# A longer gather ring, smaller count low parts and a re-ordered start of three layers in a graph network kernel

## The chip, the cores and the metric

One Trainium2 chip, one core of it. The time is device time in microseconds (us) of one execution. The engines are TensorE (PE), VectorE (DVE), ScalarE (ACT), GpSimd (POOL) and SyncE (SP); they run their own instruction streams and wait for each other on semaphores.

## The reference

625 nodes with rows of 512, 10000 edges (src, dst) sorted by dst, with a type and a weight. Four blocks, each `x = layernorm(x + block(x))`:

```python
# L0: relational, 3 edge types, 3 node types
agg = segment_sum(einsum(x, W_rel)[etype, src] + b_rel[etype], dst); h = relu(x @ W_self[ntype] + b_self[ntype] + agg)
# L1: three SAGE layers
agg = segment_sum(x[src], dst) / max(cnt, 1)
h = relu(layernorm(agg @ W_l[i].T + x @ W_r[i].T + b[i]) * g[i] + b2[i]); x = h + x
# L2: four GINE layers
m = relu(x[src] + edge_attr @ We + be); h = ((1 + eps) * x + segment_sum(m, dst)) @ W1 + b1
x = relu(relu(batchnorm(h)) @ W2 + b2)
# L3: SAGE and a gate
h = (segment_sum(x[src], dst) / max(deg, 1)) @ W_l + b + x @ W_r;  h = h * sigmoid(h)
```

## The kernel before, in words

Nodes lie in NT = 5 row tiles of R = 125. Edges lie in TE = 83 tiles of up to 128, TF = 54 of one kind and TL = 29 of another, each of which scatters to one row tile. A float32 product is made of parts: a value is split into a high part (ScalarE casts it to fp32r) and a low part (VectorE subtracts the high part from the value), and PE multiplies the parts. Weights pass through the buffer `w_stage`: SP loads a 128x512 piece, ScalarE casts it (`w_high`, L1045), VectorE makes its low part (`w_low`, L1391), both into one of two weight buffers W[0] and W[1]. SP loads the next weight's piece after the low part of the last one (`w_split`).

The stages in order, with the times of the profile:

- Set-up and the rows of the relational product, 0 to about 101 us. They are stored to HBM as `rel_rows`.
- Counts, about 101 to 153 us. PE multiplies one-hot matrices into a count matrix in PSUM: NCF = 3 blocks and then NCL = 5 blocks of tiles, 8 in all, each of which raises `c_used`. The result, copied to TC, is the adjacency matrix with counts. Its high part is AT[HI] and its low part AT[LO]. Only two blocks of 125x125 of the low part are used, and `block_max`, `block_row` and `block_words` find which. `low_blocks` (L834) transposes these two blocks through PE, the copy `count_low_blocks` (CLO, L1266) takes them to SBUF, and `mean_low` (L913) multiplies by them.
- First block, about 153 to 276 us. POOL gathers a tile's rows of `rel_rows` with one indirect DMA each (L633), in the order ORDER. ScalarE casts the gathered tile (`m_high`, L1135), VectorE subtracts (`m_low`, L1623, raises `m_made`), PE multiplies with the tile's one-hot matrix (L862, raises `m_free`). The first GA = 4 gathers land in H; the others in a ring of GR = 24 slots. Gather i of the ring waits for `m_made` of i - GR + 1; the early ones wait for `c_used` of (i + 1) // 4, since the slots overlay buffers of the count stage. Between the steps, PE multiplies x by the self weights (L797), one `fill` at a time, in the order that FILL_AT writes out, and the weights W4 to W7 are split at steps W4_AT = 4, 26, 48, 70. The one-hot matrices are made in NG = 21 groups of four tiles; groups from KEPT = 12 on are stored by ScalarE's queue (`s_store`, L1119) to HBM in this stage, for the GINE layers, and groups 0 to 11 are made again, four in each SAGE layer (`onehots_again`, L1587).
- A layer norm and SAGE layer l = 0 (276 to 341 us), layer l = 1 (341 to about 410), layer l = 2 (to 448). Per row tile: root of the variance on ScalarE (`root`, L1053, function Sqrt), reciprocal on VectorE, normalisation, transposes on PE (L663), the two weight products (L671), the bias (`z_bias`, L903), `mean_low` and the product with AT (`mean_tile`, L919, raises `o_done`). Of l = 2 VectorE makes statistics, the affine part, the residual, statistics again; then the parts of x for the GINE layers: high on ScalarE (L1278), low on VectorE (`part_low`, L1831). `set_lhs` (L1738) makes the eight chunks of a matrix that the GINE gathers use, four of them within the row tiles of l = 2.
- Four GINE layers, 448 to 905 us. Their gathers are PE products (L973) or indirect DMAs into a queue (`queue_rows`).
- Last layer, 905 to 968 us: layer norm (ScalarE waits for `w2_done` of all five tiles before it), transposes, products, means, and per tile a sigmoid on ScalarE (L1344, function Sigmoid) with the next root behind it. ScalarE loads a table (ACT_TABLE_LOAD) when the function changes from Sqrt to Sigmoid or back.

The order within an engine is that of the program; nothing is reordered.

## Time and profile before

| | |
|---|---|
| Median of 3 runs | 971.86 us (967.61 to 972.33) |
| Profiled execution | 970.5 us, span 968.6 us |
| Granted clock, mean | 0.921 |
| PE busy | 841.4 us (87% of the span), 3561 matmuls |
| VectorE busy | 712.1 us (74%) |
| ScalarE busy | 516.6 us (53%) |
| POOL busy | 281.5 us (29%) |
| First block, 153 to 276 us | PE busy 103.34 of 123 us, clock 0.91, POOL 61.16 us |
| GINE layers, 448 to 905 us | PE busy 431.51 of 457 us, clock 0.98 |

The rows of the profile below give the start and the duration of a group of instructions on one engine in us from the span's start, the line of the kernel, the output and input tiles, and in brackets the idle time of the engine before it and what ended that. "issue" means that the profile shows nothing that the engine waited for; "remote" is a releaser that it can't name. The clock of 1.0 is 2.4 GHz, of 0.50 is 1.2 GHz.

### The profile page before, as it was taken

What the parts mean: (1) busy time and instruction counts of PE and PEld (TensorE: products, weight loads), DVE (VectorE), ACT (ScalarE), POOL (GpSimd) and SP (SyncE); (2) the same over time, 40 slices, a digit from 0 to 9 for tenths busy, and PEclk for the clock granted to TensorE, in tenths of its full rate; (3) what the DMA queues carried; (4) which work ended last, traced back from release to release, by engine and by line L of the source; (5) the groups of instructions that cost most, each with busy time, mean ns of one, the idle gap of its engine ahead of it and who ended that gap; (6) DMA issues with size and microseconds to landing.
All of it is one profiled execution on the core that took longest, in us unless ns stands there. A gap on an engine that the chain in (4) does not pass through costs nothing.

```text
span 968.6 us, 13328 instructions
## 1 busy us (share of the span) xinstructions
PE 841.4 (87%) x3561; PEld 603.7 (62%) x3561; DVE 712.1 (74%) x1275; ACT 516.6 (53%) x986; POOL 281.5 (29%) x245
## 2 busy tenths in 40 slices
PE   2989779887869789995999989999999999999796
PEld 2667345655647567773665865667656766658664
DVE  8997825765876677786888668976799758986535
ACT  2376103544646241514786567755677557764445
POOL 3000653865200000015352075502654045520000
PEclk9989657989969799997999999999999999999898
DMA  5412454676433312208676077841978138860101
GB/s 113 142 38 87 115 161 154 178 225 193 151 99 157 129 45 64 84 26 217 148 187 180 3 202 179 200 119 33 240 177 217 37 108 197 178 165 1 43 1 53
DMA packets 59286, 122.20 MB, mean 126 GB/s; under 512 B 9096, under 2 KB 22698, under 8 KB 59221
## 3 DMA queue, kind: packets, MB, share of 16 engines
q0 software_dynamic: 20048, 52.18, 22.6%
q1 hardware_dynamic: 36581, 64.56, 22.6%
q10 hardware_dynamic: 2592, 4.61, 1.3%
q8 instruction: 38, 0.62, 0.3%
q14 instruction: 27, 0.22, 0.1%
HBM read 105.60 MB, written 15.73 MB: 125 GB/s over the span
## 4 chain that ended last, share of the span: by engine, by line
PE 67%; DVE 17%; ACT 8%; issue 5%; another core or an unknown queue 2%; DMA 1%; SPq 0%; ACTq 0%; DVEq 0%
PE ps L996 15%; PE ps L973 10%; PE ps L671 9%; PE ps L1012 6%; PE ps L1028 6%; PE ps L797 4%; PE ps L862 3%; PE ps L919 3%; PE ps L776 2%; PE ps L663 2%; ACT slot_recs L1090 2%; PE ps L765 2%; DVE z_parts L1864 1%; DVE w L1391 1%
## 5 line engine op out<-in xcount | busy, mean ns | idle before, releaser
L996 PE MATMUL ps<-z_parts,onehot_dst 128*125 128x512 f32 x664 | 205.2, 414 | 5.6 <-DVE z_parts L1864 2.9
L1864 DVE SCALAR_TENSOR_TENSOR z_parts<-ps,z_parts 128x512 fp32r<-128x512 f32 x216 | 147.9, 688 | 43.4 <-ACT z_parts L1296 31.0
L671 PE MATMUL ps<-w,xT 128*125 128x512 f32 x660 | 174.7, 419 | 5.1 <-DVE w L1391 5.1
L1296 ACT ACTIVATE z_parts<-ps 128x512 fp32r<-128x512 f32 x216 | 128.7, 597 | 80.9 <-PE ps L973 66.9
L973 PE MATMUL ps<-x_parts,gather_lhs 128*128 x432 | 142.4, 415 | 22.5 <-DVE x_parts L1831 12.1
L996 PEld LDWEIGHTS ps<-z_parts,onehot_dst 128*125 128x125 f32 x664 | 110.0, 186 | 72.8 <-issue 55.0
L671 PEld LDWEIGHTS ps<-w,xT 128*125 128x125 f32 x660 | 129.8, 200 | 37.7 <-issue 6.8
L639 POOL DMA_INDIRECT queued<-node_rows,srci x60 | 96.0, 1600 | 93.7 <-ACT queued L1245 76.8
L653 POOL TENSOR_TENSOR work<-x_cur,be_rows 125x512 f32<-125x512 f32 x20 | 25.5, 1282 | 317.7 <-ACT x_cur L1059 188.9
L973 PEld LDWEIGHTS ps<-x_parts,gather_lhs 128*128 128x128 f32 x432 | 80.3, 193 | 56.5 <-issue 40.2
L633 POOL DMA_INDIRECT gathered<-rel_rows,rowi x79 | 85.7, 1084 | 51.4 <-DVE gathered_parts L1623 22.0
L1864 DVE SCALAR_TENSOR_TENSOR z_parts<-queued,z_parts 128x512 fp32r<-128x512 f32 x116 | 79.6, 686 | 5.5 <-ACT z_parts L1296 4.6
L1623 DVE TENSOR_TENSOR gathered_parts<-gathered,gathered_parts 128x512 fp32r<-128x512 f32 x79 | 53.1, 689 | 36.1 <-ACT gathered_parts L1135 26.2
L1135 ACT CAST gathered_parts<-gathered 128x512 fp32r<-128x512 f32 x79 | 47.5, 618 | 49.4 <-PE ps L862 34.6
L1296 ACT ACTIVATE z_parts<-queued 128x512 fp32r<-128x512 f32 x116 | 72.5, 625 | 0.4 <-issue 0.2
L862 PE MATMUL ps<-gathered_parts,onehot_dst 128*125 128x512 f32 x166 | 56.6, 440 | 16.5 <-DVE gathered_parts L1623 12.2
L644 POOL DMA_INDIRECT queued<-node_rows,srci x56 | 58.6, 1046 | 17.1 <-issue 12.2
L797 PE MATMUL ps<-w,xT 128*125 128x512 f32 x180 | 55.4, 422 | 3.2 <-DVE eps_deg L1600 1.8
L1012 PE MATMUL ps<-x_parts,w 128*128 128x312 f32 (+1 forms) x384 | 58.0, 313 | 0.1
L1391 DVE TENSOR_TENSOR w<-w_stage,w 128x512 fp32r<-128x512 f32 x88 | 57.0, 686 | 1.4 <-ACT w L1045 1.3
L1012 PEld LDWEIGHTS ps<-x_parts,w 128*128 128x128 f32 x384 | 57.1, 194 | 1.0 <-issue 1.0
L1028 PE MATMUL ps<-w,xT 128*125 128x512 f32 x240 | 57.0, 397 | 0.0
(275 smaller groups left out, 1154.7 us busy)
## 6 DMA issues: line engine op xcount, KB each, us to landing
w_stage<-in_weights SPq DMA_DIRECT2D x88, 256.0 KB
onehot_dst<-onehot_rows SPq DMA_DIRECT2D x80, 250.0 KB
onehot_rows<-onehot_dst ACTq DMA_DIRECT2D x18, 250.0 KB
gather_lhs<-edge_src_rows SPq DMA_DIRECT2D x8, 432.0 KB, 7.4
node_rows<-work SPq DMA_DIRECT2D x20, 160.0 KB, 2.0
queued<-node_rows,srci POOLq DMA_INDIRECT x116
node_rows<-work SPq DMA_DIRECT2D x20, 90.0 KB, 2.0
rel_rows<-rel_rows_out SPq DMA_DIRECT2D x10, 160.0 KB, 1.9
```

What stands on the lines that cost most here:

```text
L633: gp.indirect_dma_start(G[place(i)][:, :], None, xr_d, bass.IndirectOffsetOnAxis(ap=rowi[:, t:t + 1], axis=0)).then_inc(gath[place(i)], 16)
L639: gp.indirect_dma_start(Q[k % QR][:, :], None, xb_d, row, compute_op=ALU.add)\
L671: mm = pe.matmul(ps[0:R, bank, :], lt[:, a, k, n * R:(n + 1) * R], w[:, b, k, :], start=first and k == 0 and (a, b) == THREE[0], stop=last ...
L797: mm = pe.matmul(ps[0:R, FBANK[i % 3], :], XT[:, a, k, n * R:(n + 1) * R], W[(NREL + t) % 2][:, b, k, :], start=k == 0 and (a, b) == THREE ...
L862: mm = pe.matmul(ps[0:R, d, :], S[:, i // SK % SR, i % SK, :], M[:, i % MR, a, :], start=False, stop=False, skip_group_check=True)
L973: mm = pe.matmul(ps[:, 5 + t % 3, :], L[:, t, :], XS[:, a, bass.ds(s, 1), :], start=a == HI, stop=a == LO)
L996: mm = pe.matmul(ps[0:R, d, :], S[:, j // SK % SR, j % SK, :], Z[:, g % ZR, a, :], start=False, stop=False, skip_group_check=True)
L1012: mm = pe.matmul(ps[:, HBANKS[i], 0:HC[h]], W[0][:, a, k, o * P:(o + 1) * P], GT[:, b, k, HC[0] * h:HC[0] * h + HC[h]], start=k == 0 and ( ...
L1028: mm = pe.matmul(ps[0:R, n, :], XT[:, a, k, n * R:(n + 1) * R], W[1][:, b, k, :], start=False, stop=k == KT - 1 and (a, b) == THREE[-1])
L1296: nc.scalar.activation(Z[:, g % ZR, HI, :], of, ACT.Relu).then_inc(z_hi, 1)
L1391: v.tensor_tensor(W[j % 2][:, LO, k, :], WS[:, k, :], W[j % 2][:, HI, k, :].bitcast(F32), ALU.subtract).then_inc(w_split, 1)
L1864: v.scalar_tensor_tensor(out=Z[:, g % ZR, LO, :], in0=of, scalar=0.0, in1=Z[:, g % ZR, HI, :].bitcast(F32), op0=ALU.max, op1=ALU.subtract) ...
```

## The change

- The first GA = 12 gathers get places of their own, four in H and eight in the weight buffer W[0] (of GR = 30 ring slots, six more lie in the region of AT). The first twelve share a semaphore in pairs. Gathers whose slot is free before the counts end wait for `c_used` of i // 5; the six in AT's region wait for all 8 count blocks; the first that waits for `m_made` is the one at i = 42.
- W4's split begins at step 14 of the first block (W4_AT), with a wait of ScalarE for twelve gathers subtracted.
- KEPT = 9: nine one-hot groups are made again, three in each SAGE layer, and three more are stored during the first block.
- The whole low part of AT is no longer made. `low_blocks` transposes two blocks of the counts themselves (TC, bank 6) and two of the high part (bank 7), four matmuls, and VectorE makes CLO from them by a copy and a subtraction, right after `w_lows(8)`. `low_blocks` comes before `z_bias`.
- `set_lhs` of chunks 4 to 7 moves from the row tiles of l = 2 to the end of l = 1, between the calls y(2, 2), y(2, 3) and y(2, 4).
- At the end of l = 2 ScalarE casts tiles 0 to 3 before the last tile's second root, and VectorE makes the low part of tile 0 before the last tile's scale.
- A spare Sqrt on one column stands ahead of the first layer norm, a spare Sigmoid behind each root of the last tiles.
- ScalarE's wait for `w2_done` ahead of the last layer norm is gone.
- The queue's landings in the GINE layers use the gathers' semaphores.

```diff
...
 NCL = -(-TL // CL)
-GA = 4
-GR = 24
+GA = 12
+GR = 30
+GX = 3
 MR = 4
...
 AHEAD = 2
-KEPT = 12
+KEPT = 9
 MADE = [KEPT * i // NL1 for i in range(NL1 + 1)]
 DEG_AT = 4
-W4_AT, W5_AT, W6_AT, W7_AT = 4, 26, 48, 70
+W4_AT, W5_AT, W6_AT, W7_AT = 14, 26, 48, 70
 FILL_AT = [0] + [6 + j * 62 // 14 for j in range(1, NREL * NT)]
...
         G += [at(g_at, 2048 * (i if i < 7 else 9), f"gathered{13 + i}", [P, D]) for i in range(8)]
-        G += [at(x_at, 2048 * i, f"gathered{21 + i}", [P, D]) for i in range(GR - 21)]
-        G = [at(h_at, 2048 * (i + 1), f"first_gathered{i}", [P, D]) for i in range(GA)] + G
+        G += [at(x_at, 2048 * i, f"gathered{21 + i}", [P, D]) for i in range(GX)]
+        G += [at(a_at, 2048 * i, f"gathered{21 + GX + i}", [P, D]) for i in range(GR - 21 - GX)]
+        G = [W[0][:, i // KT, i % KT, :].bitcast(F32) for i in range(2 * KT)] + G
+        G = [at(h_at, 2048 * (i + 1), f"first_gathered{i}", [P, D]) for i in range(NT - 1)] + G
+        assert len(G) == GA + GR and 2048 * (GR - 21 - GX) <= APAD * 4
         assert AHEAD * 4096 <= 4 * CG * P and MR * 4096 <= g_off and g_off + 2048 * 13 <= 52224 and TF * P * 4 + 2048 * (QR + 2) <= 52224
...
         xr_last = sem("last_rel_rows_stored")
-        gath = [sem(f"gathered{i}_in") for i in range(GA + GR)]
+        gath = [sem(f"gathered{i}_in") for i in range(GA // 2 + GR)]
         m_hi = sem("m_hi")
...
         TCK = TC[:, :, :].rearrange("p s (d n) -> p (s d) n", n=R)
-        ATL = AT[:, LO, :, :].rearrange("p s n -> p (s n)").bitcast(F32)
+        ATH = AT[:, HI, :, :].rearrange("p s n -> p (s n)").bitcast(F32)
+        TCF = TC[:, :, :].rearrange("p s n -> p (s n)")
         TCB = TC[:, :, :].rearrange("p s (d n) -> p (s d) n", n=R)
...
 
+        def arrival(i):
+            return i // 2 if i < GA else GA // 2 + (i - GA) % GR
+
+        def queue_landed(l, k):
+            before = (TE - GA - 1 - k % QR) // GR + 1
+            return 16 * (before + l * ((TL - 1 - k % QR) // QR + 1) + k // QR + 1)
+
         def landed(i):
-            return 16 if i < GA else 16 * ((i - GA) // GR + 1)
+            return 32 if i < GA else 16 * ((i - GA) // GR + 1)
 
...
                     gp.wait_ge(m_made, i - GR + 1)
-                elif i >= 3:
-                    gp.wait_ge(c_used, min((i + 1) // 4, NCF + NCL - 1))
+                elif i >= GA + 21 + GX:
+                    gp.wait_ge(c_used, NCF + NCL)
+                elif i >= 4:
+                    gp.wait_ge(c_used, min(i // 5, NCF + NCL - 1))
                 gp.indirect_dma_start(G[place(i)][:, :], None, xr_d,
-                                      bass.IndirectOffsetOnAxis(ap=rowi[:, t:t + 1], axis=0)).then_inc(gath[place(i)], 16)
+                                      bass.IndirectOffsetOnAxis(ap=rowi[:, t:t + 1], axis=0)).then_inc(gath[arrival(i)], 16)
             def queue_rows(l, k):
...
                 pe.wait_ge(low_made, 3)
-                pe.wait_ge(at_made, NT)
+                pe.wait_ge(at_hi, NT)
                 for j in range(2):
                     b = field(low_word(j), 6, 31, NB - 1)
-                    mm = pe.matmul(ps[0:R, 6, P * (j + 2):P * (j + 2) + R], ident[0:R, 0:R],
-                                   ATL[0:R, bass.ds(b * R, R)], start=True, stop=True)
+                    for bank, rows in ((6, TCF), (7, ATH)):
+                        mm = pe.matmul(ps[0:R, bank, P * (j + 2):P * (j + 2) + R], ident[0:R, 0:R],
+                                       rows[0:R, bass.ds(b * R, R)], start=True, stop=True)
                 mm.then_inc(low_done, 1)
...
                             block_row()
+                    low_blocks()
                     z_bias(l, False)
-                    low_blocks()
                     mean_low(l)
-                    pe.wait_ge(at_hi, NT)
                     for n in range(NT):
...
             def m_high(t):
-                act.wait_ge(gath[place(t)], landed(t))
+                act.wait_ge(gath[arrival(t)], landed(t))
                 if t >= MR:
...
                     nc.scalar.copy(DGR[:, :], DG[:, :]).then_inc(dgr_made, 1)
+                if t == W4_AT:
+                    act.wait_ge(m_made, GA)
                 if t in range(W4_AT, W4_AT + 8, 2):
...
                     w_high(7, (t - W7_AT) // 2)
+            nc.scalar.activation(spare[:, :], epst[:, :], ACT.Sqrt)
             act.wait_ge(deg_made, 1)
...
                 if l == 0:
-                    act.wait_ge(low_done, 3)
-                    nc.scalar.copy(CLO[0:R, :, :], ps[0:R, 6, 2 * P:4 * P].rearrange("p (j n) -> p j n", n=P)[:, :, 0:R])\
-                        .then_inc(clo_made, 1)
                     act.wait_ge(z_done, 1)
...
             top = NT * NL1
+            def part_high(n):
+                nc.scalar.copy(XS[0:R, HI, n, :], X[0:R, n, :]).then_inc(xs_hi, 1)
+
             for n in range(NT):
                 root(n, top + FIRST[n], epsd)
+                if n == NT - 1:
+                    act.wait_ge(o_done, NT * NL1)
+                    act.wait_ge(x_made, NT * NL1 + NT - 1)
+                    for m in range(NT - 1):
+                        part_high(m)
                 root(NT + n, top + SECOND[n])
                 normal(X[0:R, n, :], H[0:R, n, :], NT + n, NT + n + 1, x_made)
-            act.wait_ge(o_done, NT * NL1)
-            for n in range(NT):
-                act.wait_ge(x_made, NT * NL1 + n + 1)
-                nc.scalar.copy(XS[0:R, HI, n, :], X[0:R, n, :]).then_inc(xs_hi, 1)
+            act.wait_ge(x_made, NT * NL1 + NT)
+            part_high(NT - 1)
 
...
                     else:
-                        c = l * ((TL - 1 - (t - TF) % QR) // QR + 1) + (t - TF) // QR + 1
                         if (t - TF) % 2 == 0:
-                            act.wait_ge(q_in[(t - TF) % QR], 16 * c)
+                            act.wait_ge(q_in[(t - TF) % QR], queue_landed(l, t - TF))
                         else:
...
                             nc.scalar.activation(X[0:R, n - 1, :], ps[0:R, n - 1, :], ACT.Relu).then_inc(x_kept, 1)
-            act.wait_ge(w2_done, NT * NL2)
             normed_rows(NL1, NT * (NL1 + 2), 2 * NT, XM_L3)
...
                 root(n, NT * (NL1 + 3) + n + 1)
+                nc.scalar.activation(spare[:, :], epst[:, :], ACT.Sigmoid)
 
...
 
+            def low_rows(bank):
+                return ps[0:R, bank, 2 * P:4 * P].rearrange("p (j n) -> p j n", n=P)[:, :, 0:R]
+
             def onehots_again(g):
...
             v.sem_inc(low_made, 1)
-            for s in range(NT):
-                v.wait_ge(at_hi, s + 1)
-                v.tensor_tensor(AT[:, LO, s, :], TC[:, s, :], AT[:, HI, s, :].bitcast(F32),
-                                ALU.subtract).then_inc(at_made, 1)
-                if s == 1:
-                    v.wait_ge(low_done, 1)
-                    v.tensor_reduce(bmx[:, :], ps[0:NB, 6, 0:R], AX_X, ALU.max).then_inc(low_made, 1)
+            v.wait_ge(low_done, 1)
+            v.tensor_reduce(bmx[:, :], ps[0:NB, 6, 0:R], AX_X, ALU.max).then_inc(low_made, 1)
             block_words()
             w_lows(8)
+            v.wait_ge(low_done, 3)
+            link(v.tensor_copy(CLO[0:R, :, :], low_rows(7)))
+            v.tensor_tensor(CLO[0:R, :, :], low_rows(6), CLO[0:R, :, :].bitcast(F32), ALU.subtract).then_inc(clo_made, 1)
             for g in range(MADE[0], MADE[1]):
...
             w_lows(11)
-            for n in range(2, NT):
-                y(2, n)
+            y(2, 2)
+            set_lhs(4)
+            set_lhs(5)
+            y(2, 3)
+            set_lhs(6)
+            set_lhs(7)
+            y(2, 4)
 
...
                 stats(H[0:R, n, :], NT + n)
-                if n < NT - 1:
-                    set_lhs(LCH // 2 + n)
+                if n == NT - 1:
+                    part_low(0)
                 scale(NT + n, NT * NL1 + SECOND[n])
-            for n in range(NT):
+            for n in range(1, NT):
                 part_low(n)
...
                     v.wait_ge(web_in, 16 * (l + 1))
-                v.wait_ge(q_in[k % QR], 16 * (l * ((TL - 1 - k % QR) // QR + 1) + k // QR + 1))
+                v.wait_ge(q_in[k % QR], queue_landed(l, k))
                 v.scalar_tensor_tensor(out=Q[k % QR][:, :], in0=WEB[:, :], scalar=wt[:, TF + k:TF + k + 1],
```

## Rows read from the trace of the kernel before

**Rows 1.** Page, part 4: the chain that ended last, share of span.
```profile
PE 67%; DVE 17%; ACT 8%; issue 5%; another core or an unknown queue 2%; DMA 1%; SPq 0%; ACTq 0%; DVEq 0%
```

**Rows 2.** Timeline of PE in the first block, its three long waits.
```profile
199.18 1.21 PE L862 MATMUL ps<-gathered_parts,onehot_dst 128*125 128x512 f32 x2 [4.07 <-issue]
...
225.72 1.21 PE L862 MATMUL ps<-gathered_parts,onehot_dst 128*125 128x512 f32 x2 [4.37 <-DVE gathered_parts L1623]
...
242.47 1.21 PE L862 MATMUL ps<-gathered_parts,onehot_dst 128*125 128x512 f32 x2 [3.12 <-DVE gathered_parts L1623]
```

**Rows 3.** Timeline of PE at the low blocks of layer l=0.
```profile
317.76 1.42 PE L903 MATMUL ps<-bias_parts,deg_rows 34*125 34x512 f32 x5
319.11 0.70 PE L834 MATMUL ps<-adjT,ident 125*125 x4
325.24 1.68 PE L913 MATMUL ps<-x_parts,count_low_blocks 125*125 x2 [5.43 <-issue]
```

**Rows 4.** Timeline of PE at the first GINE gather.
```profile
448.28 1.65 PE L973 MATMUL ps<-x_parts,gather_lhs 128*128 x3 [12.05 <-DVE x_parts L1831]
```

**Rows 5.** Timeline of PE in the last layer.
```profile
907.26 0.65 PE L663 MATMUL ps<-ident,work 125*128 125x125 f32 x4 [2.45 <-ACT work L1069]
...
957.35 2.49 PE L919 MATMUL ps<-x_parts,adjT 125*125 125x512 f32 x10
```

**Rows 6.** Timeline of POOL, count stage: start, us, [idle before, releaser].
```profile
126.75 0.95 POOL L633 DMA_INDIRECT gathered<-rel_rows,rowi  x1 [0.30 <-issue]
...
150.40 0.94 POOL L633 DMA_INDIRECT gathered<-rel_rows,rowi  x1 [1.34 <-remote]
```

**Rows 7.** Page, part 5: busy, mean ns, idle before and its releaser.
```profile
L1135 ACT CAST gathered_parts<-gathered 128x512 fp32r<-128x512 f32 x79 | 47.5, 618 | 49.4 <-PE ps L862 34.6
```

**Rows 8.** Windows: us, busy us (x instructions) per engine, PEclk, DMA, GB/s.
```profile
123.00:132.00 9.00, 5.09 (x30) 3.12 (x30) 0.16 (x1) 0.95 (x2) 3.78 (x4) 0.50 0.54 157
132.00:138.00 6.00, 5.25 (x34) 3.53 (x34) 2.72 (x8) 0.00 (x0) 3.80 (x4) 0.50 0.52 145
223.00:232.00 9.00, 6.28 (x22) 4.98 (x23) 5.67 (x10) 4.63 (x9) 4.92 (x5) 0.81 0.39 117
325.30:331.00 5.70, 5.59 (x13) 4.00 (x14) 1.73 (x3) 0.76 (x2) 0.00 (x0) 0.50 0.57 184
408.00:415.00 7.00, 6.61 (x22) 5.00 (x22) 3.54 (x6) 3.05 (x5) 0.00 (x0) 0.76 0.41 150
908.00:915.00 7.00, 4.97 (x15) 4.08 (x16) 4.75 (x12) 4.95 (x9) 0.00 (x0) 0.53 0.00 0
```

**Rows 9.** Timeline of ScalarE at the first layer norm.
```profile
278.06 1.28 ACT L1053 ACT_TABLE_LOAD   x1 [5.80 <-DVE mv L1668]
```

**Rows 10.** Timeline of VectorE at the end of layer l=2.
```profile
436.11 0.70 DVE L1738 TENSOR_SCALAR gather_lhs<-gather_lhs,pidx,pone 128x864 fp32r<-128x864 f32 x1
...
441.84 0.16 DVE L1683 RECIPROCAL rstd<-sd 125x1 f32<-125x1 f32 x1 [0.36 <-ACT sd L1053]
...
443.59 3.76 DVE L1831 TENSOR_TENSOR x_parts<-x_cur,x_parts 125x512 fp32r<-125x512 f32 x5 [1.39 <-ACT x_parts L1278]
```

**Rows 11.** Timeline of ScalarE at the last sigmoid.
```profile
958.73 1.28 ACT L1344 ACT_TABLE_LOAD   x1
960.02 0.69 ACT L1344 ACTIVATE x_cur<-ps,rdeg 125x512 f32<-125x512 f32 x1
```
**Rows 12.** Timeline of ScalarE at the low blocks.
```profile
323.62 0.37 ACT L1266 CAST count_low_blocks<-ps 125x250 fp32r<-125x250 f32 x1 [11.70 <-DVE onehot_dst L1587]
```

**Rows 13.** Timeline of VectorE at y(2,3).
```profile
403.17 0.75 DVE L1677 SCALAR_TENSOR_TENSOR x_parts<-ps,rdeg,x_parts 125x512 fp32r<-125x512 f32 x1 [1.59 <-ACT x_parts L1064]
```

**Rows 14.** Timeline of ScalarE at the end of layer l=2.
```profile
442.96 2.68 ACT L1278 CAST x_parts<-x_cur 125x512 fp32r<-125x512 f32 x5
```

**Rows 15.** Timeline of VectorE ahead of the last layer.
```profile
900.73 0.18 DVE L1668 BATCH_NORM_AGGREGATE mv<-st 125x2 f32<-125x6 f32 x1
```

**Rows 16.** Timeline of ScalarE at the start of the last layer.
```profile
904.85 0.29 ACT L1053 ACTIVATE sd<-mv,epst 125x1 f32<-125x1 f32 x1 [8.47 <-PE ps L1028]
```

More of the change, by code:

```diff
@@ L275, in build @@
         zero = sb("zero", [P, P], BF16)
+        spare = sb("spare", [P, 1])
         one2 = sb("one2", [2, ND], F32R)
@@ L389, in build @@
         q_set = sem("queue_rows_set")
-        q_in = [sem(f"queue{i}_in") for i in range(QR)]
+        q_in = gath[GA // 2:GA // 2 + QR]
         x_kept = sem("x_kept")
```

3 lines of the change are left out of this document (1 added, 2 removed).

## The prediction

> **What bounds the kernel now.** I read the chain that ended last first. [rows 1] gives 67% of it to TensorE (PE) and only 17% and 8% to VectorE (DVE) and ScalarE (ACT). So a saving counts only where PE stands idle. The four GINE layers, nearly half of the span, are left as they are by the diff, and nothing is to be had there. Next I read PE's own rows for those whose bracket shows an idle time: three of 3 to 4.4 us in the first block [rows 2], 5.43 us ahead of the low blocks' product [rows 3], 12.05 us ahead of the first GINE gather [rows 4], 2.45 us at the start of the last layer [rows 5]. The diff has an edit near each. Last came the rows of the engine that each bracket names. The profiled execution took 970.5 us (span 968.6 and 1.9 around it), 1.4 under the median of 971.86. All terms are against 970.5, and 1.4 is added back at the end.
>
> **Gathers and the ring (A, 0).** Twelve gathers instead of four get landing places of their own, and the ring has 30 slots instead of 24, so 42 gathers instead of 28 can go out before the first one that waits for `m_made`. A gather costs POOL 0.95 us with 0.30 of issue, 1.25 [rows 6], so 14 are 17.5 us of POOL's time. They are worth something only where a gather is late. In the first block ScalarE's casts of gathered rows idle 49.4 us, 34.6 of it for PE [rows 7], and PE's matmuls on them name VectorE's subtraction [rows 2]; nothing names a landing. The extra lead hides what is hidden. W4 moves from step 4 to step 14, since gathers lie in W[0] until then: four casts, four subtractions and SP's four loads, with W5's loads behind them on SP's queue. The step length is 122/83, 1.5 us; W4's last part is then subtracted at step 24 and W4 is first used at step 25 or 26, so only a step or two lie between; PE takes each step after VectorE's part of it, and that order hides it. W5 is cast from step 26 as now. ScalarE's new wait at step 14 (for `m_made`) has its next casts queued behind it, and PE waits for those, but 12 subtractions are done by step 14 anyway. The three one-hot stores more are issues on ScalarE's queue in the same idle time. All this is costed at nothing; if the cover were gone, a late gather would cost up to its 1.25 us, a late weight part about one step, 1.5.
>
> What may not be free is the form of the stream. Now 15 gathers go out in a row, until 127.7 us, and after that POOL rests 1.34 us after each few [rows 6]. In the 9 us around the end of that run PE did 30 matmuls; in the next 6 us it did 34, in 5.25 us of busy time [rows 8]. At the latter's pace 30 take 5.3 us, so 3.7 us went, with the clock at 0.50 in both. The new pacing (one count block per five gathers) makes the run nearly unbroken. I take zero, as the row that names the waiter in the first block never names a gather; the bounds are 11.6 less (the first block's three waits of 4.07, 4.37 and 3.12 vanish [rows 2]) and 18 more. Both are rivals below.
>
> **Square-root table (D, -1.1).** The ACT_TABLE_LOAD at 278.06 lasts 1.28 us and stands between VectorE's first variance and the root, after 5.80 idle us [rows 9]. A spare root ahead of that wait moves the load into the idle time: 1.28 + 0.3 are hidden by 5.80, and would cost the same 1.6 if ScalarE came late. The gain is 1.28 at most, 0.6 if the root then meets VectorE inside an operation of 0.7 [rows 10]; I take 1.1. The Trainium skill, "ScalarE: Activation LUTs", section "What ACT_TABLE_LOAD costs", adds a drain of 1.38 us to each switch, 2.66 in all; by that page the gain would be about 2.5 and the sum 1.4 lower. The trace disagrees: behind the load at 958.73 the sigmoid starts at 960.02, 0.01 us after the load's end [rows 11].
>
> **Low blocks (B, -5.3).** Now: z's bias 317.76 to 319.18, `low_blocks` from 319.11, 0.70, then PE idles 5.43 until 325.24 [rows 3]. What is late is the copy of CLO, ScalarE's 0.37 us at 323.62. Its data is there at 319.81, but it stands behind the `s_store` of the fourth remade one-hot, which its bracket names [rows 12]. After: VectorE makes CLO itself, right behind w_lows(8), and three one-hots per layer instead of four come behind CLO. AT's low part on VectorE, five subtractions, is gone. `low_blocks` is four matmuls, 2 x 0.70 = 1.4, and stands ahead of z's bias. Step by step: z ends 317.8; low blocks until 319.2; copy and subtraction, 0.4 each by ScalarE's 0.37 on the same shape, until 320.0, hidden by z's bias (1.42, until 320.6). From CLO's end, 323.99, to the product PE took 1.25, so it starts at 321.2, 4.0 earlier. Bounds: 3.4, if the two operations take 0.7 each as those of 512 do, and 4.6, if PE's own 1.25 overlaps the bias. The idle time has a second price: PE's clock is 0.50 from 325.3 to 331.0, 5.7 x 0.50 = 2.85 us of work lost; after the shorter gap ahead of the same product in layer l=2 it is 0.76 over 7 us, 1.7 lost [rows 8]. So 1.2 to 1.3 more, from 0 to 2.4. Sum 5.3, from 3.4 to 7. VectorE's chain of the layer starts at the end of each tile's means, which move whole.
>
> **Layer l=2 per tile (C, -2.5).** This stretch runs at VectorE's pace. `set_lhs`, 0.70, stands in four tiles ahead of the reciprocal, but the last tile, which has none, still waits 0.36 for ScalarE's root there [rows 10]: removing it saves about 0.17 per tile, 0.7 in all. It moves to between y(2,2), y(2,3) and y(2,4), in pairs of 1.4 us, where VectorE idles 1.59 [rows 13] and then about as long again: free, but with 0.2 us to spare; uncovered, up to 1.4 per pair. At the end of the layer ScalarE now casts five tiles, 442.96 to 445.64 [rows 14], VectorE subtracts five, 443.59 to 447.35, 0.75 each [rows 10], and PE starts at 448.28 [rows 4]. After, four casts come ahead of the last tile's root and part_low(0) ahead of its scale: 0.75 in a wait of 0.36, so 0.39 late. Scaled: 442.2 + 0.39 - 0.7 = 441.9; four subtractions, 3.0, until 444.9. The fifth cast starts at 442.96 - 0.3 and ends 443.2, in time. 447.35 - 444.9 = 2.45. What could be late is the root itself, behind four casts of 0.54 on ScalarE, 2.1 us; they fit if the tile before is normalised early enough, and cost up to 2.1 if not. Bounds 0.4 and 3.2 (the subtractions follow the casts at once).
>
> **The last layer's wait (F, -3.0).** VectorE has the first tile's variance at 900.91 [rows 15], but ScalarE's root starts at 904.85, held by `w2_done` of all tiles, PE's L1028 [rows 16]. Without the wait the root runs near 901, and normalising and scaling go beside PE's product, so PE's idle 2.45 ahead of 907.26 [rows 5] goes whole. The clock from 908 to 915 is 0.53, 3.3 us lost [rows 8]; a shorter gap gives part of that back, but VectorE still makes tiles at its own pace. I take 2.45 + 0.55; bounds 1.5 (VectorE's statistics are next) and 4.
>
> **Spare sigmoid (E, +0.8).** In the final tiles ScalarE alternates between two tables. From the second tile on the load stands right behind the root and ends as the sigmoid begins: 958.73, 1.28, then 960.02. PE has finished the last mean tile at 959.84 [rows 5], 0.2 before, so ScalarE sets the pace. A spare activation is one more on it, 0.29 as the small root of [rows 16], some 0.2 with overlap, four times. Nothing hides it if ScalarE is the pace. Bounds 0 (the wait for VectorE's variance hides it) and 1.2.
>
> **Sum.** 970.5 - 1.1 - 5.3 - 2.5 - 3.0 + 0.8 = 959.4; + 1.4 = 960.8. With all terms at one bound: 971.9 - 4.7 = 967.2 (0.6 + 3.4 + 0.4 + 1.5 - 1.2) and 971.9 - 15.5 = 956.4 (1.3 + 7 + 3.2 + 4).
>
> **Rivals.** (1) The forecast, 956.4 to 966. Chance 0.55.
> (2) The longer run of gathers slows PE in the count stage as the first one did. 15 cost 3.7; 27 more at that rate cost 6.7: 967.5, no change. For: 30 against 34 matmuls [rows 8]. Against: PE may have waited for a row there and not for the memory. Chance 0.10. The Trainium skill, "DMA: Bandwidth & Descriptors", section "SWDGE vs HWDGE vs iDMA", says that GpSimd writes its descriptors to rings in SBUF that VectorE can lock it out of, which would hurt POOL, not PE; the rows show only that the two coincide.
> (3) The other side. Every nine gathers or so without a rest bring one stall of the kind that the first block shows, and the 27 more put three into it: 4.37 of wait and (1 - 0.81) x 9 = 1.7 of clock [rows 2, 8], 18.2 in all: 979.0, slower. It decides from 15.9 us, 5.3 each. Against: POOL runs ahead and rests there. Chance 0.05.
> (4) With the lead, POOL is never in a hurry in the first block, and the three waits vanish: 960.8 - 11.6 = 949.2. For: one of them is "issue", none a landing [rows 2], so what holds them is not in the data flow. Against: then nothing shows that it is POOL. Chance 0.15.
> (5) The gaps of PE close but open again on VectorE and ScalarE, so half of B, C and F comes: 960.8 + 5.4 = 966.2. For: C's and F's stretches are at VectorE's pace. Against: at B what follows is released by PE. Chance 0.15.
>
> **Range and chances.** The likeliest time is 960.8. The range goes from 949.0 (rival 4) to 967.5 (rivals 2 and 5); beyond it lie rival 3 and the outer parts of 2 and 4. A change of 0.5%, 4.9 us, is about what can be told from none: faster is below 967.0, slower above 976.7. Faster: 0.55 + 0.15 + 0.12 of rival 5 + 0.03 of rival 2 = 0.85; same 0.10; slower 0.05.
>
> **What would show it.** In the profile after: no table load between the first variance and its root; the low blocks' product with an idle of about 1 us and a clock above 0.6 behind it; the first GINE gather with an idle near 9.5; the last layer's first transpose with no idle; the final tiles 0.2 us longer each. The prediction is wrong if the count stage or the first block moves by more than 3 us: a slower PE from 120 to 150 (2, 3), or the three waits gone (4).

## The result and the profile after

The changed kernel takes 958.57 us (median of 4 runs, 953.77 to 961.46); the kernel before took 972.10 us beside it. The ratio is 0.988, with a 95% interval of 0.984 to 0.992, so 8 to 16 us came off. The profile below is of an execution of 953.77 us (span 951.9), the fastest of the four. It is 16.7 us shorter than the profiled one of before, more than the medians differ by, so a second trace of the same kernel (span 957.4 us) stands beside it from here on.

First the chain that ended last, share of the span, of the changed kernel:

```profile
PE 70%; DVE 16%; ACT 7%; issue 6%; DMA 0%; ACTq 0%; SPq 0%; DVEq 0%
```

PE's share rose from 67% [rows 1] to 70%; the gaps went and the work stayed. This table gives the stages between marks of PE's timeline in the traces, in us:

| Stretch, from PE's marks | before | after | after, 2nd trace |
|---|---|---|---|
| second part of the counts: its first matmul to the first scatter | 35.64 | 41.66 | 43.92 |
| first block: first to last scatter | 116.07 | 106.30 | 114.75 |
| last scatter to the low blocks' product | 50.39 | 43.56 | 43.82 |
| low blocks' product to the last mean of l=0 | 15.60 | 13.44 | 13.41 |
| layers l=1 and l=2 to their last mean | 95.39 | 94.84 | 95.20 |
| last mean of l=2 to the first GINE gather | 12.05 | 9.87 | 9.91 |
| GINE layers, to the end of the last weight product | 456.53 | 458.13 | 452.64 |
| from there to the first mean of the last layer | 32.13 | 27.88 | 27.41 |
| means of the last layer | 22.90 | 22.90 | 22.90 |
| last mean to the end | 8.76 | 9.13 | 9.14 |

Every stretch with an edit moved, and so did two that the forecast had at zero: the counts got 6 to 8 us longer and the first block 1 to 10 us shorter. The GINE layers, where nothing was changed, differ by 5.5 us between two traces of the same program; all fourteen traces lie between 452.5 and 458.1. That much is chance there, and the rest of the table is to be read with it in mind.

The low blocks on PE, in the changed kernel:

```profile
312.89 0.38 PE L849 MATMUL ps<-counts,ident 125*125 x2
...
313.85 1.43 PE L918 MATMUL ps<-bias_parts,deg_rows 34*125 34x512 f32 x5
315.76 0.49 PE L928 MATMUL ps<-x_parts,count_low_blocks 125*125 x1 [0.48 <-issue]
```

And on VectorE, whose two operations follow at once:

```profile
313.96 0.42 DVE L1795 CAST count_low_blocks<-ps 125x250 fp32r<-125x250 f32 x1 [1.65 <-PE ps L849]
314.41 0.42 DVE L1796 TENSOR_TENSOR count_low_blocks<-ps,count_low_blocks 125x250 fp32r<-125x250 f32 x1
```

The idle time of 5.43 [rows 3] is 0.48. Four windows of the changed kernel, beside [rows 8]:

```profile
123.00:132.00 9.00, 4.84 (x26) 2.60 (x26) 0.00 (x0) 1.14 (x2) 6.87 (x8) 0.50 0.72 212
132.00:138.00 6.00, 1.49 (x7) 0.73 (x7) 0.25 (x1) 0.00 (x0) 2.27 (x4) 0.50 0.60 173
...
315.80:321.50 5.70, 5.27 (x22) 4.02 (x23) 4.52 (x9) 2.48 (x5) 0.00 (x0) 1.00 0.68 235
...
892.00:899.00 7.00, 4.87 (x20) 3.82 (x19) 4.75 (x12) 5.01 (x9) 0.00 (x0) 0.76 0.00 0
```

Behind the low blocks the granted clock is 1.00 where it was 0.50, in the last layer 0.76 where it was 0.53. In the count stage PE did 26 matmuls in 9 us and then 7 in 6 us, where it had done 30 and 34. POOL meanwhile, in the changed kernel:

```profile
133.92 0.95 POOL L647 DMA_INDIRECT gathered<-rel_rows,rowi  x1 [0.30 <-issue]
137.99 0.97 POOL L647 DMA_INDIRECT gathered<-rel_rows,rowi  x1 [3.12 <-PE ps L790]
```

The one at 133.92 is the twentieth in a row since 104.20. POOL rests as PE's count comes late, and PE is at full pace again when POOL has rested. All this while PE's waits are "issue", so no row names what holds it.

The first block's long waits in this trace are 1.58 and 2.75 us, in place of 4.07, 4.37 and 3.12 [rows 2]:

```profile
211.13 0.72 PE L877 MATMUL ps<-gathered_parts,onehot_dst 128*125 128x512 f32 x2 [1.58 <-DVE gathered_parts L1645]
214.60 1.21 PE L877 MATMUL ps<-gathered_parts,onehot_dst 128*125 128x512 f32 x2 [2.75 <-DVE gathered_parts L1645]
```

The second trace of the same kernel has them at their old size:

```profile
208.90 1.21 PE L877 MATMUL ps<-gathered_parts,onehot_dst 128*125 128x512 f32 x2 [4.33 <-DVE gathered_parts L1645]
...
248.51 1.21 PE L877 MATMUL ps<-gathered_parts,onehot_dst 128*125 128x512 f32 x2 [3.81 <-DVE gathered_parts L1645]
```

So of the 9.8 us by which the first block is shorter in the first trace the second one keeps 1.3; what part is chance takes more traces ("The old gathers"). The first layer norm, the end of l=2 and the start of the last layer on PE, in the changed kernel:

```profile
277.94 1.09 PE L677 MATMUL ps<-ident,work 125*128 125x125 f32 x4 [2.54 <-ACT work L1083]
...
281.92 4.04 PE L685 MATMUL ps<-w,xT 128*125 128x512 f32 x12
...
433.91 2.49 PE L987 MATMUL ps<-x_parts,gather_lhs 128*128 x5 [9.87 <-DVE x_parts L1856]
...
891.88 0.59 PE L677 MATMUL ps<-ident,work 125*128 125x125 f32 x4
894.60 0.76 PE L677 MATMUL ps<-ident,work 125*128 125x125 f32 x4 [2.13 <-ACT work L1083]
```

The last layer's first transpose has no idle time (2.45 before [rows 5]); the second has 2.13, as before.

### The profile page after: what moved, and what is told of

The parts are those of the page before. It is cut to its first block, busy times and chain, and to the rows that moved or that the text cites. A ratio compares the mean times of both kernels' runs of the same rounds, so it can differ in the third digit from the quotient of the medians.

```text
span 951.9 us, 13338 instructions
## 1 busy us (share of the span) xinstructions
PE 835.9 (88%) x3565; PEld 600.8 (63%) x3565; DVE 707.6 (74%) x1269; ACT 519.1 (55%) x992; POOL 278.0 (29%) x245
## 4 chain that ended last, share of the span: by engine, by line
PE 70%; DVE 16%; ACT 7%; issue 6%; DMA 0%; ACTq 0%; SPq 0%; DVEq 0%
PE ps L1010 15%; PE ps L685 10%; PE ps L987 10%; PE ps L1026 6%; PE ps L1042 6%; PE ps L811 4%; PE ps L877 4%; PE ps L934 3%; PE ps L790 3%; PE ps L677 2%; DVE z_parts L1889 2%; PE ps L779 2%; DVE w L1410 1%; ACT z_parts L1315 1%; ACT slot_recs L1104 1%
## 5 line engine op out<-in xcount | busy, mean ns | idle before, releaser
L685 PE MATMUL ps<-w,xT 128*125 128x512 f32 x660 | 171.2, 412 | 4.9 <-DVE w L1410 4.9
L685 PEld LDWEIGHTS ps<-w,xT 128*125 128x125 f32 x660 | 126.9, 196 | 36.6 <-issue 6.6
L647 POOL DMA_INDIRECT gathered<-rel_rows,rowi x71 | 72.8, 1026 | 43.9 <-DVE gathered_parts L1645 19.5
L877 PE MATMUL ps<-gathered_parts,onehot_dst 128*125 128x512 f32 x166 | 54.5, 424 | 10.4 <-DVE gathered_parts L1645 9.6
L1645 DVE TENSOR_TENSOR gathered_parts<-gathered,gathered_parts 128x512 fp32r<-128x512 f32 x71 | 47.7, 690 | 19.2 <-ACT gathered_parts L1149 16.2
L1149 ACT CAST gathered_parts<-gathered 128x512 fp32r<-128x512 f32 x71 | 42.7, 618 | 33.9 <-PE ps L877 26.4
L1026 PE MATMUL ps<-x_parts,w 128*128 128x312 f32 (+1 forms) x384 | 60.4, 321 | 0.1
L1026 PEld LDWEIGHTS ps<-x_parts,w 128*128 128x128 f32 x384 | 59.5, 202 | 0.5 <-issue 0.5
L1059 ACT CAST w<-w_stage 128x512 fp32r<-128x512 f32 x88 | 50.5, 616 | 14.6 <-DVE onehot_dst L1606 9.9
L811 PE MATMUL ps<-w,xT 128*125 128x512 f32 x180 | 54.8, 418 | 3.2 <-DVE eps_deg L1622 1.8
```

Of the source, the lines that this page charges most:

```text
L647: gp.indirect_dma_start(G[place(i)][:, :], None, xr_d, bass.IndirectOffsetOnAxis(ap=rowi[:, t:t + 1], axis=0)).then_inc(gath[arrival(i)], 16)
L685: mm = pe.matmul(ps[0:R, bank, :], lt[:, a, k, n * R:(n + 1) * R], w[:, b, k, :], start=first and k == 0 and (a, b) == THREE[0], stop=last ...
L811: mm = pe.matmul(ps[0:R, FBANK[i % 3], :], XT[:, a, k, n * R:(n + 1) * R], W[(NREL + t) % 2][:, b, k, :], start=k == 0 and (a, b) == THREE ...
L877: mm = pe.matmul(ps[0:R, d, :], S[:, i // SK % SR, i % SK, :], M[:, i % MR, a, :], start=False, stop=False, skip_group_check=True)
L1026: mm = pe.matmul(ps[:, HBANKS[i], 0:HC[h]], W[0][:, a, k, o * P:(o + 1) * P], GT[:, b, k, HC[0] * h:HC[0] * h + HC[h]], start=k == 0 and ( ...
```

## The experiments

Four sets ran on different chips: the first four kernels on one where the kernel before took 975.0 us, the next four on one with 974.5, the three after that on one with 947.8, and the last on one with 950.7. Comparisons between kernels are made within a set, and between sets only where said.

### The changed kernel again

Edit: none.

> The changed kernel once more, for a second trace of it. Theory A (each saving lies in a stall that the edit removes): the product of the low blocks stands near 316, the first GINE gather near 434, the last transpose near 892, each within 3 us. Rival N (a part of the 16.6 us by which the two traces differ is chance of one execution): the count stage, the first block or the GINE layers differ between the two traces of the same program by 3 us or more.

Measured: 958.8 us (958.39 to 961.58), ratio to before 0.987 (0.980 to 0.995); its stages are the table's last column. The marks that the theory named lie 11, 11 and 6 us late. The 11 come from the counts and the first block, in which the second trace is 2.3 and 8.5 us longer; the third mark is back at 6 because its GINE layers are 5.5 us shorter. Rival N holds: 3 us and more of difference in the counts, the first block and the GINE layers is chance. From the last scatter to the first GINE gather the two traces agree within 0.7 us.

### The old gathers

```diff
-GA = 12
-GR = 30
+GA = 4
+GR = 24
...
-W4_AT, W5_AT, W6_AT, W7_AT = 14, 26, 48, 70
+W4_AT, W5_AT, W6_AT, W7_AT = 4, 26, 48, 70
...
-        G = [W[0][:, i // KT, i % KT, :].bitcast(F32) for i in range(2 * KT)] + G
...
-                elif i >= GA + 21 + GX:
-                    gp.wait_ge(c_used, NCF + NCL)
-                elif i >= 4:
-                    gp.wait_ge(c_used, min(i // 5, NCF + NCL - 1))
+                elif i >= 3:
+                    gp.wait_ge(c_used, min((i + 1) // 4, NCF + NCL - 1))
...
-                if t == W4_AT:
-                    act.wait_ge(m_made, GA)
```

> The changed kernel with the gathers of the kernel before (4 first places, a ring of 24, one count block per 4 gathers, W4 split from step 4). Theory A (the gather part is worth little, in both directions): 0 to 3 us slower than the changed kernel; the count stage ends near 153.5 again instead of 159.8, and the first block takes about 116 us from its first scatter instead of 106, with the three waits back. Rival (the gather part is the gain of the first block): over 6 us slower.

Measured: 957.55 us (954.42 to 960.67), ratio 0.986 (0.978 to 0.994), against 958.8 for the changed kernel on the same chip; the ranges overlap. The counts take 35.49 us and the first block 115.64, as before (35.64 and 116.07). Five traces with the changed gathers have 41.7 to 45.2 (mean 44.0) and 106.3 to 114.8 (mean 110.7). So the gather part costs 8.4 us in the counts and gives 5.2 back in the first block. It is no gain: the kernel with the old gathers was expected to be 0 to 3 us slower and is 1.3 us faster by the medians, which these runs can't tell from nothing.

### Without the spare Sigmoid

```diff
                 root(n, NT * (NL1 + 3) + n + 1)
-                nc.scalar.activation(spare[:, :], epst[:, :], ACT.Sigmoid)
```

> The changed kernel without the spare Sigmoid behind the last roots. Theory A (a spare activation is one more on the engine that sets the pace): 0.8 us faster, from the last mean product to the end 0.1 to 0.3 shorter per tile. Rival (the table load needs no successor, the spare one is what hides it): 1 to 5 us slower, 1.28 per tile.

Measured: 960.85 us (957.82 to 965.78); its range overlaps that of the changed kernel (958.39 to 961.58). The stage decides: from the last mean to the end 8.78 us against 9.13. ScalarE's timeline of the changed kernel in the last tile:

```profile
941.98 1.28 ACT L1365 ACT_TABLE_LOAD   x1
943.27 0.20 ACT L1365 ACTIVATE spare<-epst 128x1 f32<-128x1 f32 x1
943.38 0.67 ACT L1362 ACTIVATE x_cur<-ps,rdeg 125x512 f32<-125x512 f32 x1
```

From load to sigmoid it is 1.40 us; in [rows 11] 1.29. The spare one overlaps with what follows and costs 0.09 to 0.11 per tile, 0.36 in all. It has nothing to hide: the load stands at the same place without it. (This is less than the 0.8 expected, and the medians, which go the other way by 2 us, can't show it.)

### Rests between the gathers, every sixth

```diff
+                if i >= 8 and i % 6 == 0:
+                    gp.wait_ge(gath[arrival(i - 2)], landed(i - 2))
                 gp.indirect_dma_start(G[place(i)][:, :], None, xr_d,
```

> The changed kernel, in which GpSimd waits at every sixth gather for the landing of the gather two before, so that no more than six follow each other without a rest. Theory R (unbroken runs of gathers hold up the other engines): the stall of TensorE between 129 and 138 us goes (6 us), and those of the first block too (1.6, 2.8, 1.5 us of wait), 5 to 12 us faster. Rival (the stalls are the load on the DMA engines or chance): same within 2 us, the stalls stay in place or move.

Measured: 947.3 us (943.77 to 948.21), ratio 0.974 (0.966 to 0.982), 11.5 us under the changed kernel on the same chip. One of its rests on POOL:

```profile
128.55 0.95 POOL L649 DMA_INDIRECT gathered<-rel_rows,rowi  x1 [3.25 <-DMA w<-rel_rows,rowi]
```

The counts take 35.17 us (43.92 in the changed kernel on this chip), so the stall is gone but for waits of 1.24 us at the most:

```profile
123.00:132.00 9.00, 6.85 (x39) 4.05 (x39) 1.13 (x4) 1.14 (x2) 4.74 (x5) 0.50 0.50 143
132.00:138.00 6.00, 4.33 (x27) 2.71 (x26) 1.77 (x5) 0.00 (x0) 2.93 (x4) 0.50 0.68 208
```

66 matmuls in the 15 us, where the changed kernel had 33. In the first block PE has no wait above 1.9 us until 245; the steps to the sixtieth take 73.4 us, against 90.5 in the second trace and 91.7 before. Then comes a new bound. PE and ScalarE in this kernel:

```profile
249.67 1.21 PE L879 MATMUL ps<-gathered_parts,onehot_dst 128*125 128x512 f32 x2 [2.90 <-DVE gathered_parts L1647]
```

```profile
247.88 0.62 ACT L1151 CAST gathered_parts<-gathered 128x512 fp32r<-128x512 f32 x1 [2.90 <-DMA gathered<-rel_rows,rowi]
```

For the first time casts wait for landings, and the last 23 us run at half the clock (0.54, as its window from 245 to 268 shows). POOL had fallen behind by its rests and by single gathers of several times the length of 0.95:

```profile
203.22 4.50 POOL L649 DMA_INDIRECT gathered<-rel_rows,rowi  x1 [0.30 <-issue]
208.03 3.96 POOL L649 DMA_INDIRECT gathered<-rel_rows,rowi  x1 [0.30 <-issue]
```

These stand where VectorE is never idle (10.00 of 10 us from 200 to 210). Theory R holds on this chip in this much: only the stream of gathers was changed, and the stalls of PE went. The mean load on the DMA engines doesn't sort them: from 132 to 138 us it is 0.68 here, with 27 matmuls, and 0.60 in the changed kernel, with 7. But a rest also lets gathers land before the next one is issued, so whether the length of the run counts or the number of gathers under way isn't shown. Nor is a busy VectorE enough for a slow gather: 19 of this trace's gathers from 155 us on lie wholly under VectorE work, and 15 of them take 0.94 to 1.49 us. The other four, of 3.96 to 4.54, each end 0.15 to 0.16 us behind a VectorE operation that reads PSUM (L1496).

### Two edits undone

```diff
-            nc.scalar.activation(spare[:, :], epst[:, :], ACT.Sqrt)
...
+            act.wait_ge(w2_done, NT * NL2)
             normed_rows(NL1, NT * (NL1 + 2), 2 * NT, XM_L3)
```

> The changed kernel with two edits undone in stages that don't touch: no spare Sqrt ahead of the first layer norm, and the wait for all five tiles of the last GINE layer back ahead of the last layer norm. Theory (each is worth its term): from the last scatter of the first block to the low blocks' product 1.1 us longer than in the changed kernel; and the idle time of 2.4 us ahead of the last layer's first transpose back, with last transpose to last mean product 1 to 2 us longer by the clock. Rival (half of it forms again on VectorE and ScalarE): 0.5 and 1.2.

Measured: one execution of 961.95 us. From the last scatter to the low blocks' product 45.58 us, 1.8 to 2.0 more than in the two traces of the changed kernel, but the other kernels with the spare root and CLO in its new place lie between 43.70 and 44.81, so 0.8 to 1.9 (1.4 against the mean of the eleven traces). Part of this is plain in all traces: from the end of the last scatter to the first transpose that PE waits for it is 6.91 us in this kernel and in the one before, and 5.74 to 5.75 in ten of the twelve with the spare root (6.24 in the two whose first block ends with waits for landings). The rows of this kernel:

```profile
287.15 1.10 PE L677 MATMUL ps<-ident,work 125*128 125x125 f32 x4 [3.47 <-ACT work L1083]
...
291.13 4.88 PE L685 MATMUL ps<-w,xT 128*125 128x512 f32 x12
```

The idle time alone misleads: it is 3.47 here and 2.54 in the changed kernel's first trace, but 3.12 in its second, since the products ahead of it vary. So does the weight product, 4.88 here and 4.04 to 5.24 with the spare root. The last layer's part: from the last weight product to the first mean 30.85, against 27.88 and 27.41, with the idle time of 2.45 back:

```profile
899.78 1.09 PE L677 MATMUL ps<-ident,work 125*128 125x125 f32 x4 [2.45 <-ACT work L1083]
```

The stretch varies between 26.4 and 29.2 in the twelve traces without the wait, and the two with it, 30.85 and 32.13, lie outside. Against the mean of the twelve, 27.9, the wait costs 3.0 us here; one trace leaves this open between 1.7 and 4.5.

### The corrections late, the parts last

```diff
-KEPT = 9
+KEPT = 12
...
+            for g in range(MADE[0], MADE[1]):
+                onehots_again(g)
             v.wait_ge(low_done, 3)
             link(v.tensor_copy(CLO[0:R, :, :], low_rows(7)))
...
-            for g in range(MADE[0], MADE[1]):
-                onehots_again(g)
...
-                if n == NT - 1:
-                    act.wait_ge(o_done, NT * NL1)
-                    act.wait_ge(x_made, NT * NL1 + NT - 1)
-                    for m in range(NT - 1):
-                        part_high(m)
...
+            act.wait_ge(o_done, NT * NL1)
+            for m in range(NT):
+                act.wait_ge(x_made, NT * NL1 + m + 1)
+                part_high(m)
...
-                if n == NT - 1:
-                    part_low(0)
...
-            for n in range(1, NT):
+            for n in range(NT):
                 part_low(n)
```

> The changed kernel with KEPT = 12 and VectorE's making of the low blocks' corrections behind the four remade one-hots of layer l = 0, so behind the landing that the fourth waits for; and, in layer l = 2, the five casts and subtractions of x behind the last tile again (set_lhs stays moved). Theory: the product of the low blocks stands 4 us later against the last scatter, with a clock of 0.50 behind it, and the means of l = 0 end 6 to 8 us later; the first GINE gather stands 2 to 2.5 us later behind the last mean of l = 2. Rival (the gain of layer l = 0 came from the order of low blocks and bias and from AT's low part, not from the stores): the product is under 2 us later.

Measured: one execution of 965.75 us. VectorE waits again for the landing, and PE for VectorE:

```profile
325.41 0.68 DVE L1603 TENSOR_TENSOR onehot_dst<-iota,dlo 128x500 fp32r<-128x500 f32 x1 [3.66 <-DMA onehot_rows<-onehot_dst]
326.01 0.41 DVE L1794 CAST count_low_blocks<-ps 125x250 fp32r<-125x250 f32 x1
```

```profile
328.07 1.68 PE L928 MATMUL ps<-x_parts,count_low_blocks 125*125 x2 [5.12 <-issue]
```

The product stands 48.56 us behind the last scatter (43.6 and 43.8 in the changed kernel) and the means end 15.29 behind it (13.4): 6.6 to 6.9 in all, the expected 6 to 8. So the place behind the stores was nearly the whole cost; the order of low blocks and bias and AT's low part, which stayed changed here, are worth no more than the 1 us by which the kernels vary in this stretch. The end of l=2 takes 11.41 us, against 9.87 and 12.05 before: casting and subtracting early is worth 1.5 us (2 to 2.5 were expected), the moved `set_lhs` 0.6.

### A rest at every tenth gather

```diff
-                if i >= 8 and i % 6 == 0:
+                if i >= 10 and i % 10 == 0:
```

> As the kernel with paused gathers, but a rest at every tenth gather instead of every sixth. There, the stalls went but the last 20 steps of the first block waited for landings. Theory R (a run above some ten gathers stalls the others, and rests cost GpSimd time that the end of the block lacks): no stall over 2 us in count stage and first block, no landing waited for, 2 to 6 us faster than with a rest at every sixth. Rival (stalls set in below ten): small stalls of 1 to 2 us at each run's end, and no gain over the other.

Measured: 955.84 us (948.66 to 962.01), ratio 0.981 (0.971 to 0.990). The counts take 43.02 us, as long as without rests, and the first block 116.90, 6 us longer than in the two kernels without rests on this chip (110.2 and 110.9). The rival holds in that nothing is gained; its stalls of 1 to 2 us are too small, for in the first block PE waits 5.54 us at 174.60, the longest such wait of all traces. The windows of this kernel:

```profile
123.00:132.00 9.00, 7.37 (x46) 4.66 (x46) 2.53 (x7) 1.14 (x2) 4.42 (x6) 0.50 0.50 141
132.00:138.00 6.00, 3.16 (x18) 1.69 (x17) 0.33 (x1) 0.00 (x0) 4.78 (x5) 0.50 0.69 186
```

POOL rests until 126.62 and then issues ten. PE is at its best behind the rest (46 matmuls) and down to 18 from 132 on, with the sixth of the run at 133.46. So a rest doesn't give credit for ten.

### Rests in the counts only

```diff
-                if i >= 8 and i % 6 == 0:
+                if 8 <= i < GA + GR and i % 6 == 0:
```

> The changed kernel with a rest at every sixth gather only among the first 42, those issued ahead of the block's ring. Theory R: the count stage ends 6 us earlier than in the changed kernel, the first block keeps its three stalls, in sum 5 to 8 us faster. Rival (a stall in the count stage is made up or comes later): same within 2 us.

Measured: 955.99 us (953.52 to 959.76), ratio 0.983 (0.976 to 0.990). The counts take 35.02 us, 8 to 10 less than the others on this chip, and the first block 116.93, with waits of 2.06 to 3.04 us in it. What was won before the block is in part lost in it: 151.95 us for both together, 154.9 to 155.3 in the two kernels with the changed gathers on this chip, 151.1 with the old ones on the other. Neither theory had this; the sum is not known better than the chance of the first block allows.

### Shorter rests, rests until gather 60, a rest at every eighth

Edits to the kernel with a rest at every sixth gather, one for each of the three kernels:

```diff
-                    gp.wait_ge(gath[arrival(i - 2)], landed(i - 2))
+                    gp.wait_ge(gath[arrival(i - 4)], landed(i - 4))
...
-                if i >= 8 and i % 6 == 0:
+                if 8 <= i < 62 and i % 6 == 0:
...
-                if i >= 8 and i % 6 == 0:
+                if i >= 8 and i % 8 == 0:
```

> As the kernel with a rest at every sixth gather, but GpSimd waits for the landing of the gather four before instead of two, so the rests are shorter (about 1 us instead of 2.3). Theory R1 (the length of the run is what counts, and a rest of 1.3 us breaks it, as the kernel before shows between its groups of four): no stall over 2 us, fewer landings waited for at the end, 0 to 8 us faster than with the longer rest. Rival R2 (a rest helps only when most gathers have landed, since what is in flight holds up the others): the stalls are back, 5 to 11 us slower than with the longer rest.

> The rests of 2.3 us at every sixth gather up to the sixtieth only; the last 23 gathers go without one. Theory R: the last 20 steps of the first block wait less for landings, but one stall of 3 to 4 us can come back there; 2 us slower to 5 us faster than with rests to the end. Rival (the landings were late because VectorE's load makes single gathers 4 us long, not for the rests): the end of the block is the same.

> A rest of 2.3 us at every eighth gather. Rests at every sixth took the stalls away and at every tenth did not. Theory R: runs of eight lie near the edge; if they are short enough, 0 to 5 us faster than at every sixth, with fewer landings waited for; if not, the count stage takes 5 us longer, as at every tenth.

Measured, with the kernel before at 947.75 us (944.69 to 954.03) on this chip: 931.26 us (ratio 0.980, 0.975 to 0.985), 934.38 us (0.985, 0.979 to 0.991) and 943.18 us (0.993, 0.989 to 0.997). These don't tell short from long rests, since on this chip the kernel before already lacks 27 us. The kernel with short rests had twelve gathers in a row from 190.22 to 204.45, and eighteen from 125.96 to 148.10 with no rest above 0.31, and no stall: its counts take 32.06 us and its first block 97.67. Its windows:

```profile
123.00:132.00 9.00, 7.48 (x44) 4.50 (x44) 2.11 (x7) 1.14 (x2) 6.41 (x7) 0.50 0.67 189
132.00:138.00 6.00, 5.40 (x35) 3.61 (x35) 2.97 (x8) 0.00 (x0) 4.49 (x5) 0.50 0.70 206
```

So on this chip a long run of gathers doesn't stall PE. The kernel with rests until gather 60 shows it best: from 211.06 on it has 23 gathers in a row, and from 210 to 240 PE does 126 matmuls in 29.68 busy us at a clock of 1.00, with the DMA engines busy 0.81 of the time. The same rests, of the longer kind, give counts of 35.17 us on the first chip and 32.00 here, so on the first chip they don't take the whole loss away. The slowest of the three, with rests of eight, has its loss at the end of the block, where a cast waits 7.25 us for a landing: there the rests only cost.

### Short rests and no spare Sigmoid

Edit: that of the short rests, and the spare Sigmoid gone.

> The changed kernel with a short rest at every sixth gather (wait for the landing of the gather four before) and without the spare Sigmoid. The three runs before this were on a chip on which the kernel before takes 948 us instead of 975, so the question of short against long rests is open; this is decided by the stages if the kernel before takes about 973 again here. Theory R1 (the length of the run counts): from the first rest-bound count matmul to the first scatter about 35 us and the first block near 100 to 108 us, 943 to 950 us in all. Rival R2 (a rest helps only when most gathers have landed): 42 us or more and 110, and 955 to 960 us.

Measured: 931.65 us (929.4 to 934.52), ratio 0.9805 (0.977 to 0.984), with the kernel before at 950.73. Again a chip of the faster kind, so the question of short against long rests stays open. Counts 32.21, first block 97.76, tail 8.78.

## Why the prediction was right, point by point

Forecast 960.8 us in 949 to 967.5, measured 958.6. The sum of 11.1 us less stands against 13.5 by the medians and 12 by the ratio. It was right in size, though two errors of opposite sign are in it: the gathers, put at nothing, cost 1 to 3 us, and the other terms gave 3 to 4 us more than their 11.1. That these nearly cancel is luck.

- **Gathers (A, 0).** The step that failed is "I take zero" for the form of the stream; by the prediction's own sign, a move of more than 3 us in either stage, this part was wrong. "The extra lead hides what is hidden" held: no cast waited for a landing. But rival 2 came true beside it, with 8.4 us in the counts (it had 6.7 and a chance of 0.10), and about half of rival 4's size, 5.2 of its 11.6 us, though the waits did not vanish. Together 3 us slower in the traces, 1 by the medians. Rests between gathers took the stall of the counts away in two kernels out of two at every sixth gather and not at every tenth, so the cause lies in POOL's stream of gathers, on the chips where it happens; what in the stream it is, its length or the gathers under way, is not shown. The Trainium skill, "DMA: Bandwidth & Descriptors", section "SWDGE vs HWDGE vs iDMA", has VectorE in its 2-port mode lock GpSimd out of its descriptor rings, and says nothing of GpSimd holding up PE. The gathers of 4.50 and 3.96 us while VectorE was never idle would agree with it, but no row shows that mode, and 15 gathers under an equally busy VectorE were not held up. What carries the stall from POOL to PE stays open.
- **Root table (D, -1.1).** The way from the last scatter to the first waiting transpose went from 6.91 to 5.75 us, by 1.16, as forecast. Behind it the first weight product took 4.99 us before and 4.04 in the first trace, which would make 2.0; the other kernels show 0.8 to 1.9 in all, so what the clock adds is small and not settled. By the drain that the Trainium skill, "ScalarE: Activation LUTs", section "What ACT_TABLE_LOAD costs", adds to each switch, the load alone would have been worth an estimated 2.5. The traces disagree: they show the 1.16.
- **Low blocks (B, -5.3).** Measured from the end of z's products, the low blocks' product came 4.7 us earlier (7.42 to 2.71; 4.0 forecast). The two operations took 0.42 each as put, `low_blocks` took 1.03 instead of 1.4, and of PE's own 1.25 most lay under the bias, the case of the bound of 4.6. Behind it came 2.2 more through the clock (1.2 to 1.3 forecast), 6.9 in all, near the upper bound. PE's idle time fell to 0.48 and its clock did not fall at all: 1.00 in the window. The gap of layer l=2 (clock 0.76) was the wrong row to size it by, since its gap is longer (1.23 us).
- **Layer l=2 (C, -2.5).** 2.2. `set_lhs` gave 0.6 (0.7 forecast) and, at its new place, fitted into VectorE's waits of 1.59 and 2.02 with 0.32 and 0.74 left. The five parts gave 1.5 (1.8 forecast), for the four subtractions took 3.56 us together and not 3.0; one of them alone took 1.76, for which no row gives a reason.
- **Last layer (F, -3.0).** 4.3 and 4.7 against before, above the bound of 4; 3.0 by putting the wait back, against the mean. The idle time of 2.45 went, the second tile's 2.13 stayed, and the clock rose from 0.53 to 0.76, which gave back more than the 0.55 put for it.
- **Spare sigmoid (E, +0.8).** +0.36. An activation behind another one of the same table costs a tenth of a microsecond here, not two.
- **Rival 5** is refuted: B and F came whole, C nearly so. Rival 3 did not come; the stall in the counts was 8.4 us and stood alone.

## What to carry to other kernels

Look, in a trace, for a stretch in which every engine is slow and no row names a reason, and see which engine alone keeps an unbroken rhythm through it; giving that engine a rest is a cheap test. Here, on one chip of the slower kind, it took 11.5 us off the changed kernel where the change's whole gather part took none. A gap in front of PE costs its length and then the clock: closing the one at the low blocks from 5.43 to 0.48 us gave 4.7 us and 2.2 more behind it. And take two traces of the same program before a difference of a few us in one stage is explained.

## What the runs showed of the hardware

- Chips differ. The kernel before took 975.0 and 974.5 us on two (and 972.1 in the result's own runs), and 947.8 and 950.7 on two others. The 27 us are of the size of its stalls in the counts and the first block (3.7 and 11.6 of waits, and the clock behind them), and on a fast chip the first block has none in three kernels of four, the fourth waiting for a landing; no trace of the kernel before was taken there, so this is only argued. It fits that on those chips the two kernels with short rests gain 2.0% on it, 16 to 19 us, about what B, C, D and F come to in the first trace (6.9 + 2.2 + 2.0 + 4.3 = 15.4), so that the rests themselves may be worth nothing there; the kernel with rests until gather 60 gains 13 us and that with a rest at every eighth 5.
- A gather on POOL lasts 0.95 us and 0.30 of issue, but some last 3.96 to 4.54 while VectorE has no idle time, and most under the same condition don't (15 of 19 in the kernel with a rest at every sixth).
- Two traces of one program differ by 8.5 us in one stage, while another hardly varies between programs: the means of the last layer take 22.90 to 22.94 in all fourteen traces.
